# Projection stage of a four-layer graph network: the softmax division on ScalarE instead of VectorE, and the first scatters' rows loaded before the next tables' weights

## What is computed

```
w    = ex / denom[dst]                                   # softmax over the edges of a node
agg  = segment_sum(w[:, :, None] * V[src], dst)          # sums by node and head
out  = msgs.reshape(N, H * D) @ Wo + bo                  # layer 1: output projection
y    = out + node_features                               # node_features is h of layer 1
x    = x + (y - mean(y)) / sqrt(var(y) + 1e-5) * gamma + beta
h    = maximum(layernorm(x), 0)                          # input of layer 2
q, k, v = h @ Wq + bq, h @ Wk + bk, h @ Wv + bv          # layer 2: own query, table of keys and values
```

## Time and profile before

| | us |
|---|---|
| median of three runs | 3891.11 |
| lowest and highest | 3884.87, 3893.51 |
| the profiled execution | 3890.64 |
| its span | 3888.9 |

### The profile page before, as it was taken

The page is one execution under the profiler, slowest core; times in us unless marked ns, Lnnn a source line. Parts: engine busy times, 40 slices in busy tenths (PEclk is TensorE's granted clock), DMA queues, the critical chain, the costliest instruction groups (busy, mean ns, idle before and its releaser), DMA issues. The chain is left out here.

```text
span 3888.9 us, 59566 instructions
## 1 busy us (share of the span) xinstructions
PE 2771.6 (71%) x13639; PEld 1620.0 (42%) x13639; DVE 2915.7 (75%) x6788; ACT 940.1 (24%) x2734; POOL 2594.1 (67%) x2675
## 2 busy tenths in 40 slices
PE   5445789999998899699999977799999640000007
PEld 4335533333332688456666644466665420000004
DVE  7897648888897334299999967599999766666664
ACT  0011112222221232245545422122222120000004
POOL 0386567777776477677777747577777447777772
PEclk8555699999999899799999989899999865555559
DMA  4487437777776433377777732688887424444440
GB/s 200 131 261 233 118 115 208 210 209 210 211 226 177 81 68 68 84 211 211 212 212 211 210 85 76 171 239 238 239 237 234 126 74 108 108 109 108 108 103 34
DMA packets 430094, 629.44 MB, mean 162 GB/s; under 512 B 254381, under 2 KB 290834, under 8 KB 428832
## 3 DMA queue, kind: packets, MB, share of 16 engines
q0 software_dynamic: 168064, 505.00, 45.7%
q1 hardware_dynamic: 252608, 94.37, 9.7%
q10 hardware_dynamic: 9312, 28.71, 2.3%
HBM read 549.09 MB, written 78.40 MB: 161 GB/s over the span
## 5 line engine op out<-in xcount | busy, mean ns | idle before, releaser
L1291 POOL DMA_INDIRECT edge_ring<-tab,edge_rec x480 | 476.0, 992 | 160.8 <-issue 136.2
L2353 POOL DMA_INDIRECT state<-tab,edge_rec x480 | 453.9, 946 | 156.9 <-issue 145.9
L1979 PE MATMUL edge_psS<-edge_terms,ident 128*128 128x256 f32 x1952 | 472.3, 386 | 19.1 <-DVE edge_psS L2023 18.7
L2525 PE MATMUL gate_psT<-ident,gate_hb 128*128 128x128 f32 x50 | 9.9, 286 | 612.1 <-ACT gate_hb L2486 612.1
L1979 PEld LDWEIGHTS edge_psS<-edge_terms,ident 128*128 128x128 f32 x1952 | 360.7, 192 | 201.1 <-DVE edge_psS L2023 154.3
L1859 POOL DMA_INDIRECT state<-tab,edge_rec x360 | 340.4, 946 | 122.7 <-issue 106.9
L1859 POOL DMA_INDIRECT state<-tab,edge_feat x360 | 340.4, 946 | 121.5 <-issue 107.1
L1358 PE MATMUL edge_psX<-state,ident 128*128 x720 | 374.4, 630 | 33.7 <-DVE edge_ring L1393 33.3
L1393 DVE TENSOR_TENSOR edge_ring<-edge_psX,edge_ring 128x1024 f32<-128x1024 f32 x240 | 292.7, 1220 | 79.4 <-DMA edge_ring<-tab,edge_rec 37.7
L1998 PE MATMUL edge_psX<-state,ident 128*128 128x512 f32 x720 | 344.6, 602 | 6.9 <-DMA state<-tab,edge_feat 4.5
L2055 DVE TENSOR_TENSOR edge_prod<-edge_psX,state 128x1024 f32<-128x1024 f32 x240 | 293.9, 1225 | 6.8 <-issue 2.3
(11 more groups left out here) (499 smaller groups left out, 6099.6 us busy)
## 6 DMA issues: line engine op xcount, KB each, us to landing
sorted_d<-state SPq DMA_DIRECT2D x8, 2312.0 KB
feat_d<-state SPq DMA_DIRECT2D x32, 528.0 KB, 5.5
edge_feat<-sorted_d SPq DMA_DIRECT2D x116, 136.0 KB
edge_feat<-feat_d SPq DMA_DIRECT2D x113, 132.0 KB
state<-tab,edge_rec POOLq DMA_INDIRECT x840
state<-src_rows ACTq DMA_DIRECT2D x26, 512.0 KB
state<-low_rows ACTq DMA_DIRECT2D x26, 512.0 KB
edge_ring<-tab,edge_rec POOLq DMA_INDIRECT x600
```

Source lines behind the costliest of these rows:

```text
L1291: pool.indirect_dma_start(out=ring[:, k, s, :], out_offset=None, in_=S["tab0"][:, :], in_offset=bass.IndirectOffsetOnAxis(ap=rec[:, k, R_S ...
L1979: last = pe.matmul(so_far, S["ident"][:, :], terms[:, s, :], start=False, stop=(s == QE - 1), skip_group_check=True)
L2353: pool.indirect_dma_start(out=ring[:, k, s, :], out_offset=None, in_=S["tab3"][:, :], in_offset=bass.IndirectOffsetOnAxis(ap=rec[:, k, R_S ...
```

## The change

The division moves to ScalarE: for each block four activations, one for each head, that multiply 64 columns by that head's reciprocal, one value for each partition. VectorE computes the reciprocals as before and tells ScalarE by a new semaphore, `shares_ready`. ScalarE divides blocks 0 and 1 before its first copy, block 2 after it, and block i + 3 at the end of round i. On SP, the loads of the first five scatter groups go before `N.load`, the other 19 after it.

```diff
     def load(self, sp):
+        self.load_first(sp)
+        self.load_more(sp)
+
+    def load_first(self, sp):
         sp.wait_ge(self.cleared, 1)
-        for g in range(self.groups):
+        for g in range(self.ring):
+            self.load_group(sp, g, g)
+
+    def load_more(self, sp):
+        for g in range(self.ring, self.groups):
             k = g % self.ring
-            if g >= self.ring:
-                sp.wait_ge(self.stored[k], g // self.ring * (16 * HERE))
+            sp.wait_ge(self.stored[k], g // self.ring * (16 * HERE))
             self.load_group(sp, k, g)
...
+        s_rl = ph.sem("shares_ready")
...
+                scattered.load_first(sp)
                 N.load(sp)
-                scattered.load(sp)
+                scattered.load_more(sp)
                 N.store_dummy(sp)
...
+                def normalise(b):
+                    for h in range(heads):
+                        own = S["big"][:, b, D + h * (D // heads):D + (h + 1) * (D // heads)]
+                        last = act.activation(own, own, ACT.Copy, scale=rl[:, b, h:h + 1])
+                    last.then_inc(s_n, 1)
+
+                act.wait_ge(s_rl, 1)
+                normalise(0)
+                normalise(1)
                 turned(0)
+                normalise(2)
                 for i in ROUNDS:
...
                         N.find_h(act, i - 2)
+                    if i + 3 < NB:
+                        normalise(i + 3)
...
-                step(dve.reciprocal(rl[:, :, :], S["l"][:, :, 0:heads]))
-
-                def normalise(b):
-                    acc = S["big"][:, b, D:D2].rearrange("p (h d) -> p h d", h=heads)
-                    dve.tensor_tensor(acc, acc, bc(rl[:, b, :], 2, [P, heads, D // heads]), ALU.mult).then_inc(s_n, 1)
-                normalise(0)
-                normalise(1)
-                normalise(2)
+                dve.reciprocal(rl[:, :, :], S["l"][:, :, 0:heads]).then_inc(s_rl, 1)
...
-                    if i + 3 < NB:
-                        normalise(i + 3)
```

## The result

| | us |
|---|---|
| changed kernel, median of 12 runs | 3897.12 |
| kernel before, median of 12 runs beside it | 3891.68 |
| ratio | 1.0018, 95% interval 1.001 to 1.0026 |
| the changed kernel's profiled span | 3892.6 |

The medians differ by 5.4 us; the ratio, which is taken over all runs, stands for 7.0 us (3.9 to 10.1 us by its interval). Both are under the 0.2% named in the prediction, but the interval does not include 1: the change makes the kernel slower.

What follows compares the result with a forecast made beforehand. The projection stage was taken as bound by a loop of waits through VectorE, ScalarE and TensorE. Late weights +5.3 us, all other terms 0, gave 3896.4 us from the median of 3891.11, range 3887.5 to 3903.

Steps and rivals of the forecast that it cites:

- The loop of waits sets the turn: Projection stage: VectorE's `new_x`, ScalarE's copy, TensorE's products, VectorE again; 6.27 us a turn, 7.94 at half clock, 28 rounds.
- The division leaves VectorE: VectorE's rounds: 25 divisions of 419 ns go and become idle time, 0; bound on the other side 10.5 us.
- The division comes to ScalarE: End of ScalarE's round: four activations a block, 1.1 us, fit in 4.21 us idle before the square root, 0.
- The added wait at the start: ScalarE before its first copy: first output block 0.7 to 1.1 us later, covered by the weights' wait, 0; uncovered 1 us.
- The last weight lands 2.8 us after its issue: Weight loads at the stage's start: last issued at 2276.3, landed about 2279.1; upper bound 5.0 us after issue.
- Shift of `new_x`: VectorE, block 1: `new_x` begins 5.3 us later through late weights, carried to the end; bounds 1.5 to 10.0 us.
- TensorE's clock: Stage start at the low clock before and after: 0, but each further round at the low level costs 1.67 us.
- Scatters' start: GpSimd's first scatter about 8 us earlier, ending as more waiting for VectorE: 0; a gain of 8 us were scatters the bound.
- Rival 1: Row loads on SP ahead of the weights are hidden: no net change, about 3891 us; chance 0.14.
- rival 3: Weights at the upper bound (+10.0 us), or +5.3 with two more low-clock rounds (+3.3): 3900 to 3901 us; chance 0.25.
- rival 4: ScalarE becomes the bound through the division: +17 us, 3908 us; chance 0.02.
- Rival 2: GpSimd or VectorE was the bound: 8 us of earlier scatters or up to 10.5 us of divisions off, 3881 to 3883; chance 0.07.

Runs made afterwards that it cites:

- the loads alone: Kernel before with five groups of row loads ahead of the weights, division still on VectorE: 3894.31 against 3885.33 us, ratio 1.0025.
- the loop cut: Kernel before with ScalarE's copy for the next tables put ahead of the square root that waits for `new_x`: 3871.50 against 3887.52 us, ratio 0.9958.
- the division alone: Changed kernel with the loads in the old order, division on ScalarE: 3889.04 against 3885.33 us, ratio 1.0005.

## Why the prediction was right, and where its terms were off

The prediction said +5.3 us by VectorE's wait for late weights, and everything else 0. The wait is the cause, as the loads alone show, and the sum came out. Point by point:

- *The loop of waits sets the turn.* Shown, by the loop cut: the stage fell from 193.8 to 177.7 us, some 10 of the 16 us by the slow turns that went with the loop. The loop turns 24 times between the 25 rows (164.3 us), not 28 times; the sum doesn't use that count.
- *The division leaves VectorE: 0.* Right; the division alone has a ratio of 1.0005 with 1 in its interval. The waits in the fast rounds went from the 0.85 us of the earlier trace rows to 1.19, the value of the earlier trace rows.
- *The division comes to ScalarE: 0, four activations 1.1 us.* Right, 1.05 us, with 3.25 us of idle time behind it in the fast round. The rule that multiplications belong on VectorE (the Trainium skill, ScalarE: Activation LUTs, Rules for kernel authors) agrees with the prices, 1.05 against 0.42 us, but did not decide the time, because ScalarE had it to spare.
- *The added wait at the start: 0, covered.* Right, and without that cover it was 0.1 us (the division alone: VectorE's scaling at 12.75 us, before 12.65), not the 1 us stated.
- *SP holds the weights back by 10.27 us.* Right in size: 11.03 us (2256.20 to 2267.23).
- *The last weight lands 2.8 us after its issue.* **This term was mis-sized: it was 6.24 us.** I had taken the price of `Wo`, a load of 128 x 2 different rows, for loads of which four read one row 128 times. The 5.0 us of the earlier trace rows, which I kept as the upper bound, were the better row. Reading one row again and again accounts for 2.2 us of the difference in one pair of profiles, scatters beside it for 0.4, which is within the spread; the rest is open.
- *Shift of `new_x`, +5.3 us.* It was +9.3 us (24.5 against 15.2 us into the stage): 3.4 us more from the landing and 0.8 from SP, within the stated 1.5 to 10.0.
- *TensorE's clock: 0.* In the profiled execution it gave 1.8 us back, one slow turn fewer; with the loads alone it did not (164.9 us from the first row to the last, before 164.3). So the 0 stands, within one turn. But *a different number of rounds at the low clock* was one of the signs of being wrong, and it came.
- *Scatters' start: 0.* Right for the changed kernel: held back by 14.5 us, the stage grows by 1.1 us, less than one slow turn. The first scatter came 6.5 us earlier, not 8.

So the stage grew by 7.35 us where 5.3 were forecast, and the medians by 5.4 us, with an interval that holds both. That the difference of the medians hits the forecast to 0.2 us is luck: the shift of `new_x` was forecast 4.0 us short (the wait 2.7 us short, 8.36 against 5.6), 1.8 us came back by a slow turn fewer, and the rest lies within the runs' spread. Of the signs of being right, the wait (4 to 6 us) and the stage (about 5 us longer) fell outside; the first weight's issue, the 1.19 us before the rows, the turns of 6.3 and 7.9 us and the short activations came as stated.

Rival 1 (hidden loads) fell with the wait of 8.36 us; half of rival 3 held (weights near the upper bound), without its slow rounds; rival 4 fell with the 4.87 us of idle time. Rival 2 fell too, but its condition, "only if L1532 waits for a store and not for L1577", named what the kernel needs to be for this change to pay: it came true once the loop was cut, and then the earlier scatters gave 5.3 to 5.5 us and the division nothing.

## What to carry to other kernels

When a stage's engines are all partly idle, look for a loop of waits through the engines' written orders before moving work between them: here one statement that waits stood ahead of one that needn't, and exchanging them gave three times what the change cost (16.0 against 5.4 us by the medians). Moving a load ahead on a queue moves every load behind it back by its issue time, so ask for the first instruction that waits for those, and price the landing by a load of the same pattern, not of the same size. Work taken off an engine that waits anyway only lengthens its wait; test it again after the bound has moved.

## What the runs showed that I had not expected

Seven loads of 1.25 MB in all landed 9.4 us after the first one's issue; in the last 4.6 us of that the DMA engines' share stood at 0.94 and they moved 128 GB/s, after 293 GB/s. With 128 different rows in place of one row 128 times it was 7.2 us, at 314 and then 256 GB/s. Issuing the weights from ScalarE's queue did not bring the rows forward: the first scatter came 0.9 us earlier, not 7, and SP's own issues grew to 1.75 us. And GpSimd's 96 scatters took 151 us from the first to the last before, 166 us after the change and 152 to 155 us with the loop cut: before, it started late and up to 126 us into the stage it hardly waited for a row of VectorE's; after, started early, it waited 5.9 us for the first row already, at 32 us, and from there on had VectorE's pace.
